# Two Flamingo blocks, 64 sequences on one core: a loop ordered anew on all five streams, eight batches deep instead of six

## What is computed

```
x = x + tanh(g_xattn[0]) * attention_0(ctx, ctx, layernorm(x))        # 16 heads, softmax over the heads
x = x + tanh(g_ffn[0])   * down(silu(gate(n)) * up(n)), n = layernorm(x)   # 768 hidden columns
x = x + tanh(g_xattn[1]) * attention_1(layernorm(x), ctx)             # 16 heads, one shared key and value head
x = x + tanh(g_ffn[1])   * (layernorm(x) @ (W + low-rank).T + b)
```

## Time and profile before

| what | value |
|---|---|
| median of 3 runs (lowest to highest) | 2441.13 us (2436.21 to 2443.69) |
| the profiled execution: its own time | 2435.5 us |
| its span in the profile | 2433.5 us |
| busy share of the span: PE, PEld, DVE, ACT, POOL | 96%, 85%, 91%, 71%, 73% |
| mean granted TensorE clock | 0.997 |

### The profile page before, as it was taken

The page is one execution under the profiler, slowest core; times in us unless marked ns, Lnnn a source line. Parts: engine busy times, 40 slices in busy tenths (PEclk is TensorE's granted clock), DMA queues, the critical chain, the costliest instruction groups (busy, mean ns, idle before and its releaser), DMA issues.

```text
span 2433.5 us, 70142 instructions
## 1 busy us (share of the span) xinstructions
PE 2346.0 (96%) x27814; PEld 2069.6 (85%) x27814; DVE 2204.6 (91%) x3678; ACT 1719.5 (71%) x3402; POOL 1775.4 (73%) x2512
## 2 busy tenths in 40 slices
PE   6899999999999999999999999999999999999897
PEld 5788888888888888888888888888888888888786
DVE  6879999999999999999999999999999999999963
ACT  4467777777777777777777777777777777777664
POOL 3667777777787787787777777777777778777653
PEclk9999999999999999999999999999999999999999
DMA  3000010010010011011000001001001001101000
GB/s 106 25 19 29 29 33 26 29 35 24 29 35 29 24 35 30 25 32 30 29 29 30 29 29 31 28 29 35 24 29 35 24 28 35 30 24 33 17 19 15
DMA packets 74326, 73.26 MB, mean 30 GB/s; under 512 B 6555, under 2 KB 73393, under 8 KB 74290
## 3 DMA queue, kind: packets, MB, share of 16 engines
q1 hardware_dynamic: 74290, 72.75, 9.6%
HBM read 54.90 MB, written 16.78 MB: 29 GB/s over the span
## 4 chain that ended last, share of the span: by engine, by line
PE 64%; DVE 20%; ACT 7%; POOL 6%; issue 2%; DMA 0%; POOLq 0%; SPq 0%; DVEq 0%; ACTq 0%
PE work L2135 13%; PE work L2136 11%; PE work L2137 11%; DVE m L1516 6%; PE scores L2228 6%; PE scores L2238 6%; PE work L2271 5%; DVE scores L1522 4%; PE work L2174 4%; ACT e L856 3%; POOL zt L416 3%; PE scores L2217 3%; ACT xn_D L813 3%; PE work L2152 2%; PE work L2158 2%
## 5 line engine op out<-in xcount | busy, mean ns | idle before, releaser
L856 ACT ACTIVATE e<-scores 120x1024 f32<-120x1024 f32 x512 | 514.2, 1030 | 83.7 <-PE scores L2238 52.5
L2135 PE MATMUL work<-xt_hi_B,w_hi 128*128 128x256 f32 x1536 | 453.2, 295 | 4.2 <-DVE y_lo_A L1496 1.6
L2136 PE MATMUL work<-xt_lo_B,w_hi 128*128 128x256 f32 x1536 | 426.7, 278 | 0.0
L2137 PE MATMUL work<-xt_hi_B,w_lo 128*128 128x256 f32 x1536 | 426.6, 278 | 0.0
L416 POOL TENSOR_TENSOR zt<-e 120x512 f32<-120x512 f32 x256 | 328.9, 1286 | 115.8 <-ACT e L856 111.8
L410 POOL TENSOR_TENSOR h_lo<-h_f,h_hi 128x256 fp32r<-128x256 f32 x384 | 280.3, 737 | 146.3 <-ACT h_hi L806 146.2
L1516 DVE TENSOR_REDUCE m<-scores 120x128 fp32r<-120x2048 f32 x128 | 290.9, 2273 | 65.7 <-PE scores L2228 65.6
L2135 PEld LDWEIGHTS work<-xt_hi_B,w_hi 128*128 128x128 f32 x1536 | 289.5, 188 | 62.7 <-DVE h_f L1510 24.9
L1522 DVE TENSOR_TENSOR scores<-scores,m 120x1024 f32<-120x1024 f32 x256 | 302.8, 1227 | 4.3
L1534 DVE TENSOR_TENSOR e<-e,work 120x2048 f32<-120x2048 f32 x128 | 291.1, 2274 | 0.2
L2136 PEld LDWEIGHTS work<-xt_lo_B,w_hi 128*128 128x128 f32 x1536 | 289.9, 189 | 0.0
(11 more groups left out here) (256 smaller groups left out, 7283.2 us busy)
## 6 DMA issues: line engine op xcount, KB each, us to landing
x_ln<-xp SPq DMA_DIRECT2D x64, 256.0 KB, 2.7
x_res<-xp SPq DMA_DIRECT2D x64, 256.0 KB, 2.7
y<-y_out SPq DMA_DIRECT2D x64, 256.0 KB, 2.2
ctx_f_A<-cp SPq DMA_DIRECT2D x64, 128.0 KB, 2.5
ctx_f_C<-cp SPq DMA_DIRECT2D x64, 128.0 KB, 2.0
qm<-mT SPq DMA_DIRECT2D x256, 4.0 KB
e<-wi SPq DMA_DIRECT2D x3, 768.0 KB, 6.7
w_ctx<-wc SPq DMA_DIRECT2D x1, 656.0 KB
```

The lines of the kernel that those rows point to most:

```text
L856: return act.activation(e[0:SC, c, 2 * h:2 * h + 2, :, :].rearrange("p a b n -> p (a b n)"), scores[0:SC, 2 * h:2 * h + 2, :].rearrange("p ...
L2135: pe.matmul(out, a_hi, b_hi_, start=first, stop=False, skip_group_check=parts)
L2136: pe.matmul(out, a_hi, b_lo_, start=False, stop=False, skip_group_check=parts)
L2137: last = pe.matmul(out, a_lo, b_hi_, start=False, stop=end, skip_group_check=parts)
```

## The change

The work of a batch, its instructions and its buffers stay. What changes:

- DEPTH goes from 6 to 8: the loop runs 56 times, prologue and epilogue handle eight batches in flight. Within an iteration, stage A's attention takes batch t - 4 where it was t - 2, B takes t - 5 (t - 3), C's layernorm t - 6 (t - 4), D t - 7 (t - 6), the store t - 8 (t - 6).
- The order of all five lists in the loop is new, and so is the work bank of many products. The loop of PE starts at `values0` instead of at wo1. Part 4 of the gated network comes ahead of part 3, and `scores0`'s two halves of banks are treated in the other order in one place.
- Semaphores: the six parts of the gated network have their own (`G_mm0` to `G_mm5`, `G_tanh0` and so on) instead of one with six counts per iteration; some rarely needed ones are merged into `ends_pe`, `ends_act`, `ends_dve`, `ends_pool`. The start values in `given` follow.
- Prologue and epilogue are in new orders. Calls of PE's functions written there: prologue, before: 18 `gate_up`, 15 `down`, 9 `scores0`, 3 `rows_out`, 6 `queries`, 2 `key_scores`, 11 `transposes`, 137 keep_busy matmuls; after: 18, 18, 9, 5, 7, 4, 13 and 89. Epilogue, before: 18, 21, 3, 15, 6, 10, 13 and 121; after: 30, 30, 7, 19, 9, 12, 19 and 177.

```
             with nc.sync.Fori(FIRST + DEPTH, LAST + 1) as t:
-                load_x_ln(t)
-                sp.wait_ge(s["res_A"], t)
-                load_x_res(t - 2)
                 sp.wait_ge(s["v0_mm"], t)
-                load_ctx("A", t - 1)
+                load_ctx("A", t - 3)
                 sp.wait_ge(s["mT_out"], t)
                 maxima_rows()
+                load_x_ln(t)
+                load_x_res(t - 4)
+                sp.wait_ge(s["kv1_mm"], t)
+                load_ctx("C", t - 5)
                 sp.wait_ge(s["res_D"], t)
-                store_y(t - 6)
-                sp.wait_ge(s["kv1_mm"], t)
-                load_ctx("C", t - 3)
...
             with nc.tensor.Fori(FIRST + DEPTH, LAST + 1) as t:
-                pe.wait_ge(s["yC_lo"], t - 1)
-                rows_out(W[3], y_hi["C"], y_lo["C"], "wo1", False).then_inc(s["woC_mm"], 1)
...
+                pe.wait_ge(s["res_A"], t)
+                values0(W[1]).then_inc(s["v0_mm"], 1)
+                queries(W[2], "A", "q0").then_inc(s["q_mm_A"], 1)
+                pe.wait_ge(s["M0_max"], t)
+                scores0(1).then_inc(s["A1_mm"], 1)
+                pe.wait_ge(s["ln_B"], t)
+                transposes(W[0], "B").then_inc(s["T_mm_B"], 1)
+                pe.wait_ge(s["T_lo_A"], t)
+                pe.wait_ge(s["ld_ctx_A"], 16 * t)
+                keys0(W[3]).then_inc(s["ends_pe"], 1)
+                pe.wait_ge(s["T_out_B"], t)
+                maxima_transposed(W[0]).then_inc(s["mT_mm"], 1)
+                pe.wait_ge(s["T_lo_D"], t)
+                rows_out(W[1], xt_hi["D"], xt_lo["D"], "f1").then_inc(s["ends_pe"], 1)
+                pe.wait_ge(s["T_lo_B"], t)
+                pe.wait_ge(s["q_out_A"], t)
+                gate_up(W[2], 0).then_inc(s["G_mm0"], 1)
+                pe.wait_ge(s["kz0_odd"], t)
+                gate_up(W[3], 1).then_inc(s["G_mm1"], 1)
+                gate_up(W[0], 2).then_inc(s["G_mm2"], 1)
+                pe.wait_ge(s["max_rows"], 64 * t)
+                pe.wait_ge(s["A1_exp"], 2 * t + 2)
+                scores1(0).then_inc(s["T0_mm"], 1)
+                pe.wait_ge(s["f1_out"], t)
+                transposes(W[1], "C").then_inc(s["T_mm_C"], 1)
+                pe.wait_ge(s["G_h1"], t)
+                gate_up(W[3], 4).then_inc(s["G_mm4"], 1)
...
+                rows_out(W[1], y_hi["A"], y_lo["A"], "wo0").then_inc(s["woA_mm"], 1)
+                pe.wait_ge(s["res_C"], t)
+                transposes(W[3], "A").then_inc(s["T_mm_A"], 1)
                 pe.wait_ge(s["M1_max"], t)
                 key_scores(0).then_inc(s["M0_mm"], 1)
...
+                pe.wait_ge(s["ln_D"], t)
+                transposes(W[0], "D").then_inc(s["T_mm_D"], 1)
```

More of the change, by code:

```diff
@@ L219, in within @@
+        s = {n: sem(n) for n in names + list(given)}
         def within(i, n, t):
@@ new lines, in _ @@
+            act.wait_ge(s["G_h0"], LAST + 1)
+            hidden_hi(0).then_inc(s["G_hi"], 1)
+            act.wait_ge(s["T_mm_C"], LAST + 1)
+            transposed_out("C", W[3]).then_inc(s["T_out_C"], 1)
+            act.wait_ge(s["G_h1"], LAST + 1)
+            hidden_hi(1).then_inc(s["G_hi"], 1)
+            exponential(e1, 0, 1).then_inc(s["T0_exp"], 1)
+            act.wait_ge(s["ends_pe"], 3 * LAST + 5)
+            act.wait_ge(s["st_out"], 16 * (LAST + 1))
+            act.activation(y_out[:, :, :], two(W[1], NT), ACT.Copy).then_inc(s["f1_out"], 1)
@@ new lines, in _ @@
+            act.wait_ge(s["G_a0"], LAST + 2)
+            tanh(2, W[1]).then_inc(s["G_tanh2"], 1)
+            act.wait_ge(s["ends_pe"], 3 * LAST + 8)
+            act.wait_ge(s["st_out"], 16 * (LAST + 2))
+            act.activation(y_out[:, :, :], two(W[2], NT), ACT.Copy).then_inc(s["f1_out"], 1)
+            act.wait_ge(s["G_h0"], LAST + 2)
+            hidden_hi(0).then_inc(s["G_hi"], 1)
+            act.wait_ge(s["T0_mm"], LAST + 2)
+            exponential(e1, 0, 1).then_inc(s["T0_exp"], 1)
@@ new lines, in _ @@
+            act.wait_ge(s["A1_sub"], 2 * LAST + 7)
+            exponential(e0, 1, 0).then_inc(s["A1_exp"], 1)
+            act.wait_ge(s["ends_pe"], 3 * LAST + 11)
+            act.wait_ge(s["st_out"], 16 * (LAST + 3))
+            act.activation(y_out[:, :, :], two(W[0], NT), ACT.Copy).then_inc(s["f1_out"], 1)
+            act.wait_ge(s["A1_sub"], 2 * LAST + 8)
+            exponential(e0, 1, 1).then_inc(s["A1_exp"], 1)
+            act.wait_ge(s["G_mm0"], LAST + 3)
+            tanh(0, W[3]).then_inc(s["G_tanh0"], 1)
@@ new lines, in _ @@
+            subtract_max(0, 1).then_inc(s["A0_sub"], 1)
+            dve.wait_ge(s["ld_x_ln"], 112)
+            moments("A", x_ln, FIRST + 5).then_inc(s["ln_eps_A"], 1)
+            subtract_max(0, 0).then_inc(s["A0_sub"], 1)
+            dve.wait_ge(s["yA_hi"], 7)
+            low(y_lo["A"][:, :, :], two(W[1], KC), y_hi["A"][:, :, :]).then_inc(s["yA_lo"], 1)
+            dve.wait_ge(s["dn_mm5"], 7)
+            residual(x2, x1, W[0]).then_inc(s["res_B"], 1)
+            values0_out(W[3]).then_inc(s["ends_dve"], 1)
@@ new lines, in _ @@
+            hidden(5, W[3]).then_inc(s["G_h5"], 1)
+            dve.wait_ge(s["yA_hi"], 8)
+            low(y_lo["A"][:, :, :], two(W[0], KC), y_hi["A"][:, :, :]).then_inc(s["yA_lo"], 1)
+            dve.wait_ge(s["M1_mm"], 8)
+            key_max(1).then_inc(s["M1_max"], 1)
+            dve.wait_ge(s["dn_mm5"], 8)
+            residual(x2, x1, W[2]).then_inc(s["res_B"], 1)
+            dve.wait_ge(s["woA_mm"], 8)
+            dve.wait_ge(s["res_B"], 8)
+            residual(x1, x_res, W[3]).then_inc(s["res_A"], 1)
@@ new lines, in _ @@
+            low(y_lo["A"][:, :, :], two(W[1], KC), y_hi["A"][:, :, :]).then_inc(s["yA_lo"], 1)
+            subtract_max(0, 0).then_inc(s["A0_sub"], 1)
+            dve.wait_ge(s["G_tanh5"], LAST + 3)
+            gated(5, W[0]).then_inc(s["G_a5"], 1)
+            dve.wait_ge(s["G_a5"], LAST + 3)
+            dve.wait_ge(s["G_lo3"], LAST + 3)
+            hidden(5, W[0]).then_inc(s["G_h5"], 1)
+            dve.wait_ge(s["woC_mm"], LAST + 3)
+            residual(x3, x2_before, W[1]).then_inc(s["res_C"], 1)
@@ L2138, in product @@
                     first = False
-                if bias is not None:
-                    last = pe.matmul(out, bias[0], bias[1], start=False, stop=True)
                 return last
@@ new lines, in _ @@
+            down(W[2], 5).then_inc(s["dn_mm5"], 1)
+            rows_out(W[3], y_hi["A"], y_lo["A"], "wo0").then_inc(s["woA_mm"], 1)
+            pe.wait_ge(s["res_B"], LAST + 3)
+            values0(W[2]).then_inc(s["v0_mm"], 1)
+            pe.wait_ge(s["ln_D"], LAST + 3)
+            transposes(W[0], "D").then_inc(s["T_mm_D"], 1)
+            key_scores(0).then_inc(s["M0_mm"], 1)
+            keep_busy(W[1], 12)
+            pe.wait_ge(s["ln_B"], LAST + 4)
+            transposes(W[1], "B").then_inc(s["T_mm_B"], 1)
```

4044 lines of the change are left out of this document (2228 added, 1816 removed), and 12 rows, old and new, of tables (given, passing).

## The result

The changed kernel takes 2378.59 us (median of 4 runs, 2378.18 to 2379.05), the kernel before 2442.07 (4 runs, 2436.21 to 2443.69). The ratio is 0.974, 95% interval 0.973 to 0.976: 2.6% faster. The forecast was 2407 us with a range of 2382 to 2438, so the sign was right, the gain was nearly twice the forecast one, and the time lies 3.4 us under the range. The profiled execution took 2379.05 us for a span of 2377.2.

What follows compares the result with a forecast made beforehand. The loop was taken as TensorE work with little stall, PE busy 98.8%, the ends as chains with stalls. Prologue 163, loop 2010.4 and epilogue 226 gave a 2399.4 us span, 2401.4 profiled, 2407 median; range 2382 to 2438.

Steps and rivals of the forecast that it cites:

- the iteration's length: Loop: 35.9 us an iteration, between 35.5 and 36.3, times 56 gives 2010.4 us.
- The walk: Loop: new engine lists stepped against each other with old durations; y_out at 14.2 plus PE's remaining 21.4 gives 35.6 us.
- The allowance: Loop: 0.3 us an iteration added for hand-offs, raising 35.6 to 35.9 us.
- the step from the profiled execution to the median: Whole kernel: profiled execution lay 5.6 us under the median of three runs, so 2401.4 became 2407 us.
- The floor: PE in the loop: 36.15 us less avoidable stalls and one type change, 35.3 us at the least.
- the first two terms: PE in the loop: 0.5 us from the wait for xn_D and 0.15 from a stall in three gate_up.
- The third term: PE in the loop: one fewer pair of matmul type changes saves 0.2 us an iteration.
- The chain that I picked: Loop: from wo0 through DVE and ACT to y_out at 14.2 us, 0.2 late for PE's transposes of C.
- Rival B: Only the loop gains, prologue and epilogue keep 409.1 us: median 2427 us, chance 0.14.
- C: Nothing gained: y_out and near-equals replace the old stalls, 36.15 us an iteration, ends unfilled, 2441 us; chance 0.10.
- S: Loop: y_out late through ACT's queue; 1.2 us late gives 2474 us; chance 0.11.
- D: Loop: load of ctx_f_A lands later than 3.2 us, 56 us per us late, estimated 2469 at high load; chance 0.03.

Runs made afterwards that it cites:

- Run 3: Changed kernel with the transposes of D put back ahead of key_scores(0) in PE's loop: 2411.1 us, iteration 36.08 us.
- Runs 4 and 5: Changed kernel with keys_values1 ahead of the queries of C on PE, one type-change pair fewer: 2416.0 us; the same with ACT's list adapted: 2378.7 us.
- run 9: Changed kernel with the load of x_res ahead of the load of ctx_f_A on SP in the loop: 2379.2 us, iteration 35.53 us.
- run 2: Changed kernel with y_out two places later in ACT's loop, behind the third tanh and an exponential of attention 1: 2468.3 us, iteration 37.16 us.
- run 1: Changed kernel with y_out one place later in ACT's loop, behind the third tanh: 2383.0 us, iteration 35.60 us.
- Run 6: Changed kernel with 0.75 us of unread statistics work added on DVE ahead of the moments of B in each iteration: 2404.2 us.

## Why the prediction was wrong in size

**The step that failed** is the iteration's length: "A walk leaves hand-offs out, so I add 0.3: 35.9 us". The walk itself gave 35.6, and the loop takes 35.50. The allowance, 0.3 x 56 = 16.8 us, and the 0.1 by which the walk was long, 5.6 us, are the 22.4 us by which the span's sum (2399.4) missed (2377.2). I had named 35.5, the exact walk, as the lower end; it was the case. What was wrong in the reasoning: DVE's and ACT's rows were taken from start to start, so hand-offs were already in them. The parts bear this out: 10.44 and 3.51 us where the walk had 10.65 and 3.55, and 14.1 on PE where it had 14.0. That slack in several near-equal pairs does not add up to a loss while each is positive is argued, not tried.

**The second part of the miss** is the step from the profiled execution to the median, 5.6 us. The profiled execution before took 2435.5 us, less than each of the timed runs; the one after, 2379.05, lies within 0.5 us of its median. With 22.4 + 5.6 the forecast of 2407 meets the 2379 of the profiled execution. The range had a term for the iteration and for both ends, but none for this step. Either miss alone would have left the time inside the range (2384.6 or 2401.4).

**The floor.** "36.15 - 0.5 - 0.15 - 0.2 = 35.3": the first two terms add up to the 0.65 gained, but not as the sum has it. PE in the iteration before, with the two instructions of ACT that it waited for:

```profile
1037.33 1.09 PE L2217 MATMUL scores<-kz,qm 32*128 32x240 f32 x16
1038.86 0.65 PE L2174 MATMUL work<-ident,xn_D 128*128 128x128 f32 x4 [0.44 <-ACT xn_D L813]
...
1048.94 0.38 PE L2135 MATMUL work<-xt_hi_B,w_hi 128*128 128x256 f32 x1
1049.16 0.28 PE L2136 MATMUL work<-xt_lo_B,w_hi 128*128 128x256 f32 x1
1049.28 0.28 PE L2137 MATMUL work<-xt_hi_B,w_lo 128*128 128x256 f32 x1
...
1050.45 0.38 PE L2135 MATMUL work<-xt_hi_B,w_hi 128*128 128x256 f32 x1
```

```profile
1049.57 0.83 ACT L834 ACTIVATE kz<-work,key_bias,parity 128x120 f32<-128x120 f32 x2
...
1052.41 1.02 ACT L856 ACTIVATE e<-scores 120x1024 f32<-120x1024 f32 x1
```

The group ahead of the transposes of D took 1.53 us from start to start (1038.86 - 1037.33) and takes 1.03 in the changed kernel, as `key_scores` does in the earlier trace rows where nothing is waited for (1.02): 0.50, the first term. The three `gate_up` took 1053.49 - 1048.94 = 4.55 and take 1026.84 - 1022.54 = 4.30: 0.25, where the sum had 0.15. Some 0.15 of it is lost at the second of the three, which starts when kz0 is done (1049.57 + 0.83 = 1050.40), and 0.1 ahead of `scores1`, which starts when the exponential of attention 0 is done (1052.41 + 1.02 = 1053.43). The other groups together take 0.1 more than before, which leaves the 0.65. Run 3 gives 0.58 back by putting the first stall back; the other two waits are read from the trace alone and were not tried.

The third term was a misreading: it set the duration of a block's first matmul (0.31) against the mean distance of two starts (0.126). Inside a block too a matmul lasts 0.28 while the next starts 0.11 to 0.12 us later (1049.16, 1049.28). Runs 4 and 5 show that a pair fewer brings nothing. That 35.5 us is the floor is not shown: by run 9 about 0.15 us of waiting is still hidden in PE's busy 1988.00 of 1988.00, so 35.3 may be no bad estimate of it, reached by a wrong term.

**What is late next.** The chain that I picked was the right one, and its price of 56 us for each us is confirmed beyond its slack (run 2, 1.66 for a delay of 1.76). It has 0.1 us of distance in the rows and in run 2, and 0.16 of the delay of run 1 was not paid, where I had it 0.2 late. Run 6 adds that its links in front (maxima to `scores0`, low part to `keys0`) are hardly looser: 0.45 of 0.75 us is paid there.

**The ends.** Prologue 163.7 against 163, epilogue 225.5 against 226, first wo0 at 63.0 against 62. Rival B (no gain in the ends) is refuted by the 19.9 us. The depth of eight and the new orders came together, in the ends as in the loop, and no run separates them. That the earlier start of the gated network is what fills the prologue is read from the trace (`gate_up` 17 us earlier, DVE still busy for 44.38 of 50 us in that stretch) and was not undone by itself.

**Rivals.** C was wrong: PE's stalls went and no late y_out or near-equal pair took their place in full. S was wrong by its condition, not its mechanism (run 2). D was wrong as the loads landed in 2.0 us, 0.5 faster than before, at the same DMA share of 0.10; run 9 shows that its cover of 0.8 us is soon used up.
The Trainium skill, "DMA: Bandwidth & Descriptors", section "Latency and other measured facts", gives 2 us for an HBM access at high load, which by the prediction's estimate meant a landing of 4.3 us and made D right. The medians here, 2.0 us and 2.5 behind a load of 256 KB, lie far below it; how long the access itself took, no run shows.

## What to carry to other kernels

Where one engine is busy for 98% of a loop, first look for its own waits: the recorded ones, and those that only the distances from start to start show, since its busy time can cover them. Here they came to 0.75 us an iteration, and the new order won 0.65. Then walk the tightest cycle from start to start with rows of running queues. In this case the length that such a walk gave was right to 0.1 us, and the allowance for hand-offs added to it was the error; an allowance belongs in the range. When a group is moved on the bounding engine, the lists of the engines that serve it may have to move too: one copy that waits at the head of ACT's queue cost 37 us here, and its place behind the other copies brought them all back.

## What the runs showed that I had not expected

- A pair of changes between the two kinds of matmul blocks fewer brings no time: 3.79 us for the four groups either way, since what the full-precision groups gain (0.11 us) `keys_values1` loses at its new place.
- PE waited 0.2 us more in each iteration for a load, and the iteration grew by 0.03: a PE that is busy for 1988.00 of 1988.00 us still had waiting in it.
- An engine that is busy for 97% of the loop (DVE, 34.4 of 35.5 us) took 0.75 us more work for 0.12 us in one place, and for 0.45 in another.
- ctx_f_A lands in 2.0 us in the new order and took 2.5 before; with x_res issued directly ahead of it, it takes 2.5 again.
